# Attention scores on half of the array's rows each: pairs of heads in two banks, on one Trainium2 core

## The reference

```python
qkv = x @ in_proj_w.T + in_proj_b
q, k, v = heads(split(qkv))                      # (b, 16, 1024, 16)
scores = einsum('bhqd,bhkd->bhqk', q * 16 ** -0.5, k)
scores = scores + mask                           # 0 where k - q <= 64, else -1e9
out = einsum('bhqk,bhkd->bhqd', softmax(scores), v)
x = layernorm(x + out @ out_proj_w.T + out_proj_b)
x = layernorm(x + moe(x))
```

## Time and profile before

| | |
|---|---|
| median of 3 runs | 1121.51 us (1119.54 to 1123.83) |
| the profiled execution: its own time | 1122.94 us |
| its span in the trace | 1121.1 us |
| mean granted TensorE clock | 0.968 of full speed |
| projection, first maxima | 0 to some 80 us |
| rounds 0 to 3 | 80 to 246.6 us |
| rounds 4 to 15 | 246.6 to 916.6 us |
| the rest of the experts | 916.6 to 1121.1 us |

### The profile page before, as it was taken

One profiled execution on the slowest core, in us unless ns is written; L12 is line 12 of the kernel. 1 busy time (PEld: TensorE's weight loads), 2 busy tenths in 40 slices (PEclk: granted clock), 3 DMA queues, 4 the chain that ended last, 5 costly groups with the idle time before them and its releaser, 6 DMA issues.

```text
span 1121.1 us, 24687 instructions
## 1 busy us (share of the span) xinstructions
PE 997.3 (89%) x8524; PEld 573.8 (51%) x8524; DVE 820.7 (73%) x1824; ACT 623.1 (56%) x1418; POOL 461.5 (41%) x679
## 2 busy tenths in 40 slices
PE   7799998888978999998799898997899976999993
PEld 3454443334533355655465445564564555787662
DVE  6488887677788677778876798778876659456583
ACT  4335776667645665765456575754466654444322
POOL 7653211133305822321265756220465763336251
PEclk9999999899988999999999999999999988999998
DMA  5754257513302254544164775451375765999541
GB/s 182 247 191 147 80 204 263 166 48 101 95 15 82 110 105 94 140 106 86 52 127 153 161 152 141 106 122 48 90 185 124 197 143 129 194 197 236 173 149 38
DMA packets 216662, 150.73 MB, mean 134 GB/s; under 512 B 134608, under 2 KB 192720, under 8 KB 216544
## 3 DMA queue, kind: packets, MB, share of 16 engines
q1 hardware_dynamic: 204160, 116.63, 41.4%
q0 software_dynamic: 10752, 29.37, 8.3%
q10 hardware_dynamic: 1632, 3.15, 0.9%
HBM read 52.46 MB, written 70.29 MB: 109 GB/s over the span
## 4 chain that ended last, share of the span: by engine, by line
PE 57%; DVE 21%; POOL 5%; issue 5%; ACT 4%; DMA 4%; SPq 3%; DVEq 0%; ACTq 0%; POOLq 0%
PE bank L836 13%; PE bank L658 10%; PE bank L628 9%; PE bank L641 8%; DVE a_mx L1378 6%; PE bank L849 4%; PE bank L688 3%; DVE e_R L1672 3%; PE bank L792 2%; PE bank L631 2%; PE bank L742 1%; PE bank L692 1%; PE bank L861 1%; POOL a_pool L1179 1%; ACT e_R L1294 1%
## 5 line engine op out<-in xcount | busy, mean ns | idle before, releaser
L1378 DVE TENSOR_REDUCE a_mx<-bank 128x1 f32<-128x512 f32 (+3 forms) x720 | 422.1, 620 | 154.3 <-PE bank L631 98.5
L1240 ACT ACTIVATE a_PT<-bank 128x512 f32<-128x512 f32 (+4 forms) x832 | 374.7, 496 | 188.5 <-PE bank L641 185.4
L641 PE MATMUL bank<-a_QS,a_KS 113*128 113x512 f16 (+4 forms) x832 | 273.6, 336 | 22.0 <-DVE a_mx L1378 14.8
L628 PE MATMUL bank<-a_KS,a_QS 112*128 112x512 f16 (+4 forms) x832 | 262.4, 336 | 18.4 <-DVE a_mx L1378 13.8
L1129 POOL TENSOR_SCALAR_AFFINE_SELECT a_PT<-a_PT 128x256 f32<-128x256 f32 (+1 forms) x288 | 109.7, 387 | 334.1 <-ACT a_PT L1240 333.4
L658 PE MATMUL bank<-a_PT,a_VG 128*17 128x512 f32 (+4 forms) x1664 | 183.6, 514 | 4.3 <-POOL a_PT L1129 4.1
L1171 POOL DMA_INDIRECT rows<-e_XR,e_slot x112 | 111.9, 1000 | 110.6 <-DVEq L1530 82.4
L1179 POOL DMA_INDIRECT a_pool<-outs,e_slot x112 | 111.0, 991 | 82.8 <-DMA outs<-e_ys 33.7
L628 PEld LDWEIGHTS bank<-a_KS,a_QS 112*128 112x128 f16 x832 | 80.3, 99 | 123.1 <-ACT a_PT L1240 53.1
L641 PEld LDWEIGHTS bank<-a_QS,a_KS 113*128 113x128 f16 x832 | 81.4, 99 | 96.5 <-DVE a_mx L1378 36.8
L1324 ACT ACTIVATE e_tq<-bank 128x256 f32<-128x256 f32 x116 | 44.4, 384 | 140.4 <-PE bank L836 140.4
(11 more groups left out here) (176 smaller groups left out, 1313.5 us busy)
## 6 DMA issues: line engine op xcount, KB each, us to landing
outs<-e_ys SPq DMA_DIRECT2D x88, 256.0 KB
rows<-a_pool SPq DMA_DIRECT2D x48, 256.0 KB, 3.2
q_dram<-p_qk SPq DMA_DIRECT2D x16, 256.0 KB, 2.8
k_dram<-p_qk SPq DMA_DIRECT2D x16, 256.0 KB, 3.4
v_dram<-p_vs SPq DMA_DIRECT2D x8, 512.0 KB, 5.7
a_QS<-q_dram SPq DMA_DIRECT2D x64, 64.0 KB
a_KS<-k_dram SPq DMA_DIRECT2D x64, 64.0 KB
a_VG<-v_dram SPq DMA_DIRECT2D x16, 256.0 KB, 4.3
```

The lines of the kernel that those rows point to most:

```text
L628: mm = pe.matmul(ps[:, at:at + hi - lo], QS[p][0:MR, t // NT, h, t % NT * P:t % NT * P + P], KS[p][0:MR, piece, h % 2, 0:hi - lo], start=T ...
L641: pe.matmul(ps[:, 0:(qc + 1) * CH - q0], KS[p][0:MR + 1, kt // NT, h % 2, kt % NT * P:kt % NT * P + P], QS[p][0:MR + 1, qc, h, q0 - qc * C ...
L1240: act.activation(PT[(G + i) % 2][:, h, 0:w], bank("ST", G, i, h)[:, 0:w], ACT.Exp)\
L1378: dve.tensor_reduce(mx[:, piece, t // NT, heads[0]:heads[0] + n, t % NT], bank("S", G, u)[:, 0:n * w].rearrange("p (h k) -> p h k", h=n), ...
```

## The change

Each head's scores use only the 48 rows (49 with the maximum) of its own half, from row 0 for heads 0 and 1 and from row 64 for heads 2 and 3 (`lane`). QS shrinks to two planes like KS, and no zeros are written. The mask's identity and triangle are made in both halves, 64 rows each and two parts, so that a mask product becomes up to two, one per part. Heads come in the order 0, 2, 1, 3, so that neighbours lie in different halves. From round 4 on `scoresT` takes two banks and issues two heads, and `scores` takes two banks and issues two units side by side; rounds 0 to 3 issue `scoresT` and the units in turn as before. The unit of 64 columns by four heads becomes two of two heads (NU 45 to 46), and `share` deals units in pairs. The row of maxima goes in two transfers. Buffers that lay in QS move.

```diff
-MR = 112
+KR = 3 * HD
+HEADS = (0, 2, 1, 3)
...
-                n = {1: 1, 2: 2, 3: 2}.get(CH // (hi - lo), HG)
-                units += [(t, piece, lo, hi, range(h, h + n)) for h in range(0, HG, n)]
+                firsts = (0, 2) if CH // (hi - lo) > 1 else HEADS
+                n = HG // len(firsts)
+                units += [(t, piece, lo, hi, range(h, h + n)) for h in firsts]
     return units
+
+
+def lane(h):
+
+    return 64 * (h // 2)
 
...
     cols = [(qc + 1) * CH - q0 + FIXED for qc, _, q0 in SLOTS]
-    lo, hi = (NU * sum(cols[:n]) // sum(cols) for n in (slot, slot + 1))
+    lo, hi = (NU // 2 * sum(cols[:n]) // sum(cols) * 2 for n in (slot, slot + 1))
...
     ident = sb("ident", [P, P], F32)
-    QS = [sb(f"QS{p}", [P, NH2, HG, CH], F16) for p in range(2)]
+    QS = [sb(f"QS{p}", [P, NH2, HG // 2, CH], F16) for p in range(2)]
     KS = [sb(f"KS{p}", [P, NH2, HG // 2, CH], F16) for p in range(2)]
-    tri = sb("tri", [P, P], F16)
+    idb = sb("idb", [P, 2, P], F16)
+    tri = sb("tri", [P, 2, P], F16)
     mx = sb("mx", [P, 2, NH2, HG, NT], F32)
...
-            def scores(G, u):
+            def scores(G, us):
+
                 p, k = G % 2, G // 2
-                t, piece, lo, hi, heads = UNITS[u]
                 for half in range(NH2):
-                    if u == NEEDS[half]:
+                    if NEEDS[half] in us:
                         on.wait_ge(stacked[half][p], k * 128 + 128)
-                ps = take("s_first" if round_of[0] < NG else "scores", "S", G, u)
-                for n, h in enumerate(heads):
-                    at = n * (hi - lo)
-                    m0, m1 = max(lo, P * t + WIN), hi
-                    mm = pe.matmul(ps[:, at:at + hi - lo], QS[p][0:MR, t // NT, h, t % NT * P:t % NT * P + P],
-                                   KS[p][0:MR, piece, h % 2, 0:hi - lo], start=True, stop=(m1 <= m0))
-                    if m1 > m0:
-                        mm = pe.matmul(ps[:, at + m0 - lo:at + hi - lo], idb[:],
-                                       tri[:, m0 - P * t - WIN:m1 - P * t - WIN], start=False, stop=True)
-                mm.then_inc(s["s_ready"], 1)
-
-            def scoresT(G, i, h):
+                first = 2 - us[0] % 2
+                if len(us) > first:
+                    scores(G, us[:first])
+                    return scores(G, us[first:])
+                into = [take("s_first" if round_of[0] < NG else "scores", "S", G, u) for u in us]
+                for n in range(HG // 2):
+                    begun = [(ps, *UNITS[u]) for ps, u in zip(into, us) if n < len(UNITS[u][4])]
+                    for ps, t, piece, lo, hi, heads in begun:
+                        h, at = heads[n], n * (hi - lo)
+                        r = lane(h)
+                        mm = pe.matmul(ps[:, at:at + hi - lo], QS[p][r:r + KR, t // NT, h % 2, t % NT * P:t % NT * P + P],
+                                       KS[p][r:r + KR, piece, h % 2, 0:hi - lo], start=True, stop=(hi <= P * t + WIN))
+                        if n == len(heads) - 1 and hi <= P * t + WIN:
+                            mm.then_inc(s["s_ready"], 1)
+                    for part in range(2):
+                        for ps, t, piece, lo, hi, heads in begun:
+                            r, at = lane(heads[n]), n * (hi - lo)
+                            m0 = max(lo, P * t + WIN)
+                            c0, c1 = m0 - P * t - WIN, hi - P * t - WIN
+                            f0, last = max(c0, 64 * part), part == 1 or c1 <= 64
+                            if c1 > f0:
+                                mm = pe.matmul(ps[:, at + f0 - c0 + m0 - lo:at + hi - lo], idb[r:r + 64, part, :],
+                                               tri[r:r + 64, part, f0:c1], start=False, stop=last)
+                                if n == len(heads) - 1 and last:
+                                    mm.then_inc(s["s_ready"], 1)
+
+            def scoresT(G, i, ns):
                 p, k = G % 2, G // 2
                 qc, kt, q0 = SLOTS[i]
-                if kt == 0 and h == 0:
-                    on.wait_ge(negmax[qc][p], k * 16 + 16)
-                ps = take("st_first" if G < NG else "scores", "ST", G, i, h)
-                pe.matmul(ps[:, 0:(qc + 1) * CH - q0],
-                          KS[p][0:MR + 1, kt // NT, h % 2, kt % NT * P:kt % NT * P + P],
-                          QS[p][0:MR + 1, qc, h, q0 - qc * CH:CH], start=True, stop=True).then_inc(s["st_ready"], 1)
+                if kt == 0 and 0 in ns:
+                    on.wait_ge(negmax[qc][p], k * 32 + 32)
+                into = [take("st_first" if G < NG else "scores", "ST", G, i, n) for n in ns]
+                for ps, n in zip(into, ns):
+                    h = HEADS[n]
+                    r = lane(h)
+                    pe.matmul(ps[:, 0:(qc + 1) * CH - q0],
+                              KS[p][r:r + KR + 1, kt // NT, h % 2, kt % NT * P:kt % NT * P + P],
+                              QS[p][r:r + KR + 1, qc, h % 2, q0 - qc * CH:CH], start=True, stop=True)\
+                        .then_inc(s["st_ready"], 1)
 
             def weighted(G, i):
                 p = G % 2
...
                     mm = pe.matmul(otbank[32 * h:32 * h + HD + 1, q0 - qc * CH:CH], VG[p][:, kt, h:VW:HG],
-                                   PT[(p + i) % 2][:, h, 0:(qc + 1) * CH - q0], start=(kt == 0),
+                                   PT[(p + i) % 2][:, n, 0:(qc + 1) * CH - q0], start=(kt == 0),
                                    stop=(i in HALF), skip_group_check=True)
                 mm.then_inc(s["pv_done"], 1)
...
-                    for u in FIRST_S.get((c, m), ()):
-                        scores(0, u)
+                    if FIRST_S.get((c, m)):
+                        scores(0, FIRST_S[c, m])
...
-            pe.wait_ge(s["tri_done"], 2)
+            pe.wait_ge(s["tri_done"], 9)
...
-                    for u, ahead in units:
-                        if not ahead:
-                            scores(G, u)
-                        elif G + 1 < NR:
-                            scores(G + 1, u)
+                    for at in (G, G + 1):
+                        us = [u for u, ahead in units if ahead == (at > G)]
+                        if us and at < NR:
+                            scores(at, us)
 
                 for i in range(NSL):
                     rest, h2 = share(i), 2 * (G * NSL + i)
-                    for h in range(HG):
-                        scoresT(G, i, h)
-                        some_scores(rest[h:h + 1] if h < HG - 1 else ())
-                        if h == 1:
-                            fill(h2)
+                    if G < NG:
+                        for n in range(HG):
+                            scoresT(G, i, (n,))
+                            some_scores(rest[n:n + 1] if n < HG - 1 else ())
+                            if n == 1:
+                                fill(h2)
+                    else:
+                        scoresT(G, i, (0, 1))
+                        some_scores(rest[0:2])
+                        fill(h2)
+                        scoresT(G, i, (2, 3))
                     if i:
                         weighted(G, i - 1)
                     elif G:
                         weighted(G - 1, NSL - 1)
-                    some_scores(rest[HG - 1:])
+                    some_scores(rest[HG - 1 if G < NG else 2:])
...
...
             def stack(G, half):
                 p = G % 2
                 for e in range(2):
-                    for dst, src, n, both_at, one_at in ((QS[p], q_dram, HG // 2, 0, 2 * HD),
-                                                         (KS[p], k_dram, 0, HD, 0)):
+                    for dst, src, both_at, one_at in ((QS[p], q_dram, 0, 2 * HD), (KS[p], k_dram, HD, 0)):
                         at = G * (2 * HD) + e * HD
                         a = src[half, :, at:at + HD].rearrange("s d i t -> s d (i t)")
-                        to = dst[:, half, n * e:n * e + 2, :].rearrange("p i t -> p (i t)")
+                        to = dst[:, half].rearrange("p i t -> p (i t)")
                         at = 64 * e + both_at
                         sp.dma_start(to[at:at + 2 * HD], a).then_inc(stacked[half][p], 16)
                         at = 64 * e + one_at
...
                 on.wait_ge(s["mT_done"], G * NH2 + half + 1)
-                sp.dma_start(QS[G % 2][MR:MR + 1, half, :, :].rearrange("o h t -> o (h t)"), mT[half][:])\
-                  .then_inc(negmax[half][G % 2], 16)
+                for e in range(2):
+                    at, w = 64 * e + KR, HG // 2 * NT
+                    sp.dma_start(QS[G % 2][at:at + 1, half, :, :].rearrange("o h t -> o (h t)"),
+                                 mT[half][w * e:w * e + w]).then_inc(negmax[half][G % 2], 16)
 
             def load_raw(n):
...
+                        on.wait_ge(s["pv_done"], NR * NSL)
                         on.wait_ge(d["sc_done"], e - NCB + 1)
...
             pool.memset(tri[:], 0.0).then_inc(s["zeroed"], 1)
```

(28 more changed lines are left out.)

25 lines of the change are left out of this document (11 added, 14 removed).

## The result

| | before | changed |
|---|---|---|
| median | 1122.67 us (1119.54 to 1129.66, 4 runs) | 1192.70 us (1188.69 to 1194.32, 4 runs) |
| the profiled execution | 1122.94 us, span 1121.1 | 1192.74 us, span 1191.0 |
| mean granted TensorE clock | 0.968 | 0.907 |

The change makes the kernel slower: 1.0624 times the time before (1.0591 to 1.0657), 70 us. 1076 us had been forecast, with 1112 as the end of the range. Run again unchanged on another chip (`after_again`, `before_again`), the two kernels took 1190.27 and 1120.93 us; the changed one stood at 1.058 (1.0546 to 1.0613), the kernel before at 0.9987 (0.9964 to 1.0011) of itself.

A forecast was written before the change was run, and what follows sets the result against it. TensorE was taken to pace the attention rounds. Against 1122.9 us: -45 (rounds 4 to 15), -5 (rounds 0 to 3), +2 (start), +2 (small things) give 1077, shown as a 1076 us median; range 1036 to 1112.

The forecast's parts named there:

- Price of a score matmul and of a pair: Score matmuls: 0.22 us per 512 columns; a pair in two row halves costs what one does, saving 104 us.
- Rival C: Score matmuls: the halves don't run together, so borders and mask products only add, 1172 us; chance 0.08.
- Part 2, the borders: Rounds 4 to 15: 409 changes between half-row score runs and full-row fills at 0.115 us each cost 47 us.
- Rival A: Borders between row halves and the full array are free, TensorE saves 104 us: 1034 us; chance 0.15.
- TensorE's net, 4.75 us a round: Rounds 4 to 15: 104 us of streaming less 47 of borders leaves TensorE 57 us, 4.75 a round.
- A microsecond taken from TensorE is a microsecond off the time: Rounds 4 to 15: TensorE's saving counts in full in seven rounds (33 us), half in five (12), 45 us saved.
- Rival B: From round 4: pairs wait for two empty banks and VectorE's reductions, 29 of 46 us gone, 1105 us; chance 0.17.
- Rival D, the clock: A TensorE that idles more is held at 1.2 GHz in six rounds, 30 us in all, 1106 us; chance 0.05.
- Part 3, rounds 0 to 3 save 5 us: Rounds 0 to 3: chance neighbours save 18 us, 75 borders give 9 back, half the rest counts: 5 us saved.
- Part 4, the start: Start: VectorE's four memsets delay the weight split, TensorE's first matmul on it some 3 us late; +2 us.
- Part 5: Small things: maxima row in two transfers, 0.5 us or so more each time, 16 more VectorE reductions; +2 us.

The follow-up runs named there:

- e12_units_ahead: Kernel before, full rows, from round 4 two banks and two matmuls at a time, second pair of units ahead of the weighted product: 1.0036 of the kernel before.
- e13_units_ahead_halves: Changed kernel, row halves kept, with the second pair of units ahead of the weighted product: 1148.52 us, 1.024 of the kernel before.
- e1_twice: The doubled matmuls: changed kernel with every score matmul issued twice into the same bank, 1.0927 of the kernel before.
- e14_64_rows: Changed kernel using all 64 rows of each half, the added rows zeros in QS and ones in KS: 1175.25 us, 1.0472 of the kernel before.
- e5_upper_rows_only: Kernel before with its score matmuls cut to the rows from 64 on, nothing running together, heads 0 and 1 scoring zero: 1.2077 of the kernel before.
- e15_ahead_and_64_rows: Changed kernel with both mends, second pair of units ahead of the weighted product and 64 rows of each half: 1137.27 us, 1.0133 of the kernel before.
- e8_opposite_neighbours: Changed kernel, one bank at a time, old deal of units, heads ordered so scoresT and the next unit lie in opposite halves: 1166.58 us, 1.0385 of before.
- e10_all_but_halves: Everything of the change but the row halves (units, even deal, two banks at a time) on full rows: 1161.68 us, 1.0327 of the kernel before.

## Why the prediction was wrong, point by point

**Price of a score matmul and of a pair: right.** A pair of 512 columns costs 0.22 us, as taken. Rival C is out.

**Part 2, the borders: right.** 0.10 us into the fill, where 0.115 had been taken. On full rows the same border is free: in `e12_units_ahead` a fill starts 0.43 us after two full-row matmuls (833.36 to 833.79), 0.22 each. The rule cited there (the Trainium skill, TensorEngine Tiling (Array Packing), Key Properties) holds for row halves too. Rival A is out.

**TensorE's net, 4.75 us a round: right, but only where the clock holds.** Round 14 shows 4.82 less busy time between `e12_units_ahead` and `e13_units_ahead_halves`; that this is so close is in part luck, since against the kernel before it is 3.4 in the changed kernel and 3.8 in `e13_units_ahead_halves`. Over rounds 4 to 15 of the changed kernel it was 599.7 us, not near 550: matmuls at 1.2 GHz last longer, which filled up what the pairs had saved.

**"A microsecond taken from TensorE is a microsecond off the time": wrong, and the step on which the sum stood.** It was read from a busy share of 98 to 99%, with all counted in seven rounds and half in five, 45 us. Three of the seven had that share (7, 10 and 14). In rounds 12 and 15 of the kernel before it was 91%, and TensorE idled some 5 us in each, as much as in some of the five that counted half:

```profile
684.60:744.90 60.30, 54.76 (x539) 33.21 (x538) 46.04 (x107) 40.91 (x98) 21.09 (x38) 1.00 0.50 127
862.00:916.60 54.60, 49.81 (x477) 29.87 (x476) 32.52 (x78) 32.78 (x82) 41.58 (x60) 0.97 0.77 178
```

Even where the share was 99% the step failed: round 14 gave 0.6 of 4.8, and four rounds at full clock 4.1 of 19.0. The doubled matmuls put some third of their length on the time. A busy share shows that an engine hardly waits. It doesn't show how close behind the others are, and here VectorE and ScalarE hand banks back with little to spare: in rounds 4 to 15 TensorE waits 51.0 us for VectorE's maxima, 27.7 for its `e_hf` and 12.0 for ScalarE's exponential, where it was 19.2, 16.6 and 4.1.

**The order of issue: left out, put at nothing without a reason.** The prediction counted nothing for the second pair of units going behind the weighted product, though the piece of the order of round 5 shown under the change has just that: `scoresT` x2, the weighted product, then the units. Worth 2.7% on full rows and 3.4 to 3.8% on halves, some 38 to 43 us of the 70, it is the largest term. **Rival B** (0.17) named the right two engines. It looked for the price in the wait for two banks, which is about 1%, and its argument against itself, two reductions in hand when a fill begins, looked only as far as the fill: behind it come two `scoresT` and the weighted product before the next unit. Its sign, score matmuls that wait for reductions far more than now, came true: 39.3 us. The 14 us that it names for now are line 641 alone; with line 628 it was 17.3.

**Rival D, the clock (0.05, +30 us): right in kind, too light, and its cause at most a part.** It put lost clock down to idle time. The rows in use matter too (`e14_64_rows`, `e5_upper_rows_only`). The changed kernel has 150 us more at 1.2 GHz. Going from `e13_units_ahead_halves` to `e15_ahead_and_64_rows`, 68 us less of it gave 1.1% or 12 us, so about 0.2 us each; from the changed kernel to `e14_64_rows` 54 us less gave 1.1 to 1.5%, 0.2 to 0.3 us each. By these rates, an estimate from two pairs of runs, 150 us are some 26 to 45 us, as much as the halves cost or more. So the clock can be the whole price of the halves; that the borders have no part in it isn't shown.

**Part 3, rounds 0 to 3 save 5 us: wrong in sign.** Their ends moved by +7.1 (round 0) and by a further +9.9 us (rounds 1 to 3, clock 0.98 to 0.86). With opposite neighbours (`e8_opposite_neighbours`) round 3 ended at 255.8 us, with full rows and all else (`e10_all_but_halves`) at 247.2, in the changed kernel at 263.6. The price of the lower clock shows in round 1 (the one behind round 0): it took 36.6 us at 0.91 in the changed kernel, and in `e15_ahead_and_64_rows`, at full clock, 34.8, as long as the 35.0 of `e10_all_but_halves`. Borders and clock were more than what chance neighbours saved; they weren't parted further.

**Part 4, the start: right in mechanism.** TensorE's first matmul on the low weights starts at 13.87 us, 3.9 later, where 3 were said; the memsets ended at 9.78 us, where 9.5 were said, and the split itself took 3.75 us instead of 2.95. How much of it is in the 7.1 us of round 0 was not separated. **Part 5:** the wait for the row of maxima fell from 6.4 to 2.0 us where 0.5 us each more was expected; the even deal cost nothing beside the pairs.

**What is left.** With both mends the changed kernel is 1.3% over the kernel before, a span of 1136.9 us against 1121.1. Rounds 4 to 15 of `e15_ahead_and_64_rows`:

```profile
259.40:929.50 670.10, 567.99 (x5780) 300.40 (x5780) 509.34 (x1176) 393.75 (x951) 286.49 (x444) 0.94 0.46 114
```

Rounds 4 to 15 take the 670 us of the kernel before, with 41 us less of TensorE in them, and round 4 begins at 259.4 us instead of 246.6. So 13 us of the 16 lie ahead of round 4, 8 of them up to the end of round 0, and 3 behind round 15. In the rounds for which the change was made halves and full rows are level, or 2 us apart in favour of the halves (672.3 us in `e12_units_ahead`). Whether pairs in rounds 0 to 3 or a shorter start would turn it into a gain wasn't tried.

## What to carry to other kernels

Before counting a busy engine's saving in full, double its work in one run: the price of the extra time is the most that you may hope to save. Here that was run only afterwards and on the changed kernel; it gave a third, and the rounds at full clock gave a fifth. When a hand-written order is regrouped, follow each consumer's gap between two deliveries, not only the count of matmuls and waits; a long step of the same engine that slips in between shows up as idle time of both. And check what a narrower matmul does to the granted clock before counting its time.

## What was not expected of the hardware

- The granted clock went with the rows in use: 0.50 over a round in which TensorE had no gap at all, with 48 or 49 rows in its score matmuls, against 0.95 with 112 or 113 (`e5_upper_rows_only`, in which half of the score matmuls also had zeros only). Rows that only multiply zeros count: 64 instead of 48 brought the time at 1.2 GHz from 222 to 167 us (`e14_64_rows`).
- Two row halves share a pair of 512 columns in 0.22 us without loss, and the change from half rows to full rows costs 0.10 us.
